# Second attention with two turned buffers and a table of inverse denominators that the output projection multiplies by

## The reference

```python
xn = layernorm(x)
q, k, v = ...                       # [B, 32 heads, S, 64], rotary positions on a part of q and k
scores = einsum('bhqd,bhkd->bhqk', q, kf) / sqrt(64)
scores = where(causal, scores, finfo.min)
attn = softmax(scores, axis=-1)
out = einsum('bhqk,bhkd->bhqd', attn, v)
out = out.transpose(0, 2, 1, 3).reshape(b, s, 32 * 64)
return out @ o_w.T
```

## Time and profile before

| | us |
|---|---|
| three runs | 2368.79, 2372.4, 2374.82 |
| median | 2372.4 |
| the profiled execution, its own time | 2372.37 |
| its span, first to last instruction | 2370.6 |
| mean granted TensorE clock (share of full speed) | 0.966 |
| attention1 | about 1030 to 1872 |
| output1 | about 1872 to 2057 |
| feed_forward1 | about 2057 to 2371 |

### The profile page before, as it was taken

How to read it: one execution, slowest core, us unless ns; L and a number is a source line. 1 busy time by engine, 2 the same in 40 slices (tenths; PEclk the granted TensorE clock), 3 DMA queues, 4 the chain that set the end, 5 groups by cost and what they waited for, 6 DMA issues and landing times. The chain is left out here.

```text
span 2370.6 us, 54461 instructions
## 1 busy us (share of the span) xinstructions
PE 2121.0 (89%) x22256; PEld 1479.6 (62%) x22256; DVE 1544.9 (65%) x2534; ACT 874.1 (37%) x1836; POOL 480.0 (20%) x408
## 2 busy tenths in 40 slices
PE   5899969999996999958898888888888699999997
PEld 4577747777775878834444444444444588787776
DVE  4544333488884544448988899988899440377776
ACT  3322113222222310025655555655656321234443
POOL 0110111212120135510111111111111344212111
PEclk9999989999998999978999999999999899999999
DMA  4221135133325543333333343333443455320100
GB/s 156 73 84 43 53 113 202 38 111 100 109 75 196 170 150 124 112 104 77 91 98 85 87 113 100 91 100 82 101 112 82 153 196 186 124 98 19 54 1 36
DMA packets 188737, 243.00 MB, mean 103 GB/s; under 512 B 38272, under 2 KB 111296, under 8 KB 185824
## 3 DMA queue, kind: packets, MB, share of 16 engines
q1 hardware_dynamic: 187648, 239.59, 32.5%
q10 hardware_dynamic: 864, 0.21, 0.0%
HBM read 156.82 MB, written 82.90 MB: 101 GB/s over the span
## 5 line engine op out<-in xcount | busy, mean ns | idle before, releaser
L1591 ACT ACTIVATE a_prob<-ps,a_nmax 128x256 f32<-128x256 f32 (+7 forms) x512 | 377.6, 740 | 353.7 <-DVE a_nmax L1619 214.0
L1704 PE MATMUL ps<-a_kt,a_q 64*128 64x512 f32 (+5 forms) x1536 | 382.8, 540 | 86.6 <-ACT a_prob L1591 63.3
L1619 DVE TENSOR_REDUCE a_nmax<-ps 128x1 f32<-128x1024 f32 (+3 forms) x256 | 257.3, 1005 | 75.7 <-PE ps L1704 74.0
L1636 DVE STREAM_TRANSPOSE a_pt_long<-a_prob 128x512 f32<-128x512 f32 (+3 forms) x512 | 279.2, 586 | 0.0
L1704 PEld LDWEIGHTS ps<-a_kt,a_q 64*128 64x128 f32 x1536 | 144.1, 194 | 186.0 <-ACT a_prob L1591 115.9
L1718 PE MATMUL ps<-a_pt_long,a_v 32*64 32x256 f32 (+3 forms) x7808 | 229.7, 346 | 1.6 <-DVE a_pt_long L1636 0.2
L1998 DVE SCALAR_TENSOR_TENSOR f_part<-ps,f_gu_scale,f_part 128x512 f32<-128x512 f32 x264 | 184.8, 746 | 65.5 <-PE ps L2045 52.2
L1718 PEld LDWEIGHTS ps<-a_pt_long,a_v 32*64 32x64 f32 x7808 | 154.3, 132 | 105.1 <-issue 76.7
L1671 POOL TENSOR_TENSOR a_o<-a_left 128x256 f32<-128x256 f32 x128 | 90.5, 729 | 597.3 <-ACT a_left L1601 597.3
L907 POOL TENSOR_TENSOR f_hT_lo<-f_h,f_hT_hi 128x512 fp32r<-128x512 f32 x64 | 82.6, 1303 | 324.5 <-ACT f_hT_hi L890 324.5
L1701 PE MATMUL ps<-a_causal,a_identb 64*128 64x128 bf16 x1024 | 112.9, 225 | 39.2 <-ACT a_prob L1591 39.2
(11 more groups left out here) (228 smaller groups left out, 4599.0 us busy)
## 6 DMA issues: line engine op xcount, KB each, us to landing
a_q<-scratch_QT SPq DMA_DIRECT2D x512, 64.0 KB, 2.1
scratch_QT<-k_qo SPq DMA_DIRECT2D x64, 256.0 KB, 2.3
a_v<-scratch_V SPq DMA_DIRECT2D x64, 256.0 KB, 4.7
scratch_OT<-a_o SPq DMA_DIRECT2D x32, 512.0 KB, 3.3
o_of<-scratch_OT SPq DMA_DIRECT2D x32, 512.0 KB, 4.1
f_block<-in_packed SPq DMA_DIRECT2D x33, 256.0 KB, 3.4
a_kt<-scratch_KT SPq DMA_DIRECT2D x128, 64.0 KB, 4.0
f_xt_hi<-scratch_xt SPq DMA_DIRECT2D x6, 1024.0 KB, 7.7
```

Source lines behind the costliest of these rows:

```text
L1591: last = nc.scalar.activation(prob[:, n % PRING, s].rearrange("p (a w) -> p a w", w=w), SC[n % 2][:, a, 0:w], ACT.Exp, bias=nmax[:, n % 4, ...
L1619: nc.vector.tensor_reduce(nmax[:, n % 4, 0:1], SC[n % 2][:, :, 0:width(0, t)], AX.XY, ALU.max, negate=True).then_inc(maxed, 1)
L1636: last = nc.vector.transpose(pt[hf][:, lo:hi, h, t - FIRST[hf], :], src.rearrange("p (j k) -> p j k", k=32))
L1704: last = pe.matmul(sc[:, a, 0:w], q[r, slot, heads[a * hf], :], kt[r, b, keys], start=not masked, stop=True, skip_group_check=True)
```

## The change

In attention1 the division goes out of the unit. ACT copies the unnormalised outputs straight from PSUM to `o` (two copies per half, `o` has two places, no `left`), and SP stores these. DVE inverts the 32 sums of a unit at once, turns the small table (`rdenT`), and SP stores it to a new array scratch_R in memory (four small transfers a unit, `store_r`). POOL has nothing to do in this stage; the constants `ones` and `diag` are not loaded.

The long turned tiles have two places (`pt_long` for blocks 0 to 23, `pt_wide` for the rest, which only tiles 7 and 6 have), so each step's tile is turned in full two steps after its score. The rings `prob` and `q` have 4 and 3 places. The tables set short values to r = 26 to 30 (steps 2 to 6 of the next unit) and long values to 34 to 46 (steps 10 to 22 of it).

In output1 each step also loads `rd` (1795 of the new code): the two rows of scratch_R that belong to the two heads of the step, each read for 64 partitions. DVE multiplies `of` by `rd` in place (1837), and ACT's rounding and SP's next loads wait for that. The first step goes in two pieces of 512 tokens.

Most of the diff of attention1 and output1 (blank lines left out):

```diff
-QRING = 4
-PRING = 8
+QRING = 3
+PRING = 4
 FIRST = (4, 0)
 BLOCKS = (32, 16)
-FRONT, BACK, WHOLE = range(3)
-TURNS = {i + 2: [(i, FRONT)] for i in range(LONG)}
-for r, back in {5: (0,), 6: (1,), 7: (2, 3), 8: (4,), 9: (5, 6), 10: (7, 8)}.items():
-    TURNS[r] += [(i, BACK) for i in back]
-for i in range(9, LONG):
-    TURNS[i + 2] += [(i, BACK)]
-TURNS.update({i + 2: [(i, WHOLE)] for i in range(LONG, USTEPS)})
-MIDDLE = 16
-LONG_VALUES = {18 + i: range(3 * i, 3 * i + 3) for i in range(10)}
-LONG_VALUES[28] = range(30, 32)
-SHORT_VALUES = {31 + i: range(2 * i, 2 * i + 2) for i in range(8)}
-LONG_LEFT = {28: (0, 1), 29: (2, 3)}
-SHORT_LEFT = {38: (0, 1), 39: (2, 3)}
-LONG_STORE, SHORT_STORE = 34, 44
-LATEST = 45
+MAIN = 24
+LATER = 2
+SHORT_VALUES = {26: range(0, 3), 27: range(3, 6), 28: range(6, 9), 29: range(9, 13), 30: range(13, 16)}
+LONG_VALUES = {34: range(0, 2), 35: range(2, 4), 36: range(4, 6), 37: range(6, 8), 38: range(8, 10), 39: range(10, 11),
+               40: range(11, 13), 41: range(13, 15), 42: range(15, 18), 43: range(18, 21), 44: range(21, 24),
+               45: range(24, 28), 46: range(28, 32)}
+SHORT_LEFT = {31: (0,), 32: (1,)}
+LONG_LEFT = {47: (0, 1)}
+SHORT_STORE, LONG_STORE = 34, 50
+INVERT = USTEPS + 2
+LATEST = 53
...
-        diag = sb("diag", [P, 32])
-        ones = sb("ones", [P, HD1])
...
-        pt = [sb(f"pt_{s}", [P, BLOCKS[i], HQ, 4, 32]) for i, s in enumerate(("long", "short"))]
+        pt_long = sb("pt_long", [P, 2, MAIN, HQ, 4, 32])
+        pt_wide = sb("pt_wide", [P, 2, BLOCKS[0] - MAIN, HQ, 2, 32])
+        pt_short = sb("pt_short", [P, BLOCKS[1], HQ, 4, 32])
-        den = sb("den", [P, 2, 16])
-        rden = sb("rden", [P, 16])
-        spread = sb("spread", [P, HQ, 4, 32])
-        left = sb("left", [P, 4, 2, 2, 4, 32])
-        o = sb("o", [P, 2, 4, 4, 32])
+        den = sb("den", [P, 2, HQ * ST])
+        rden = sb("rden", [P, HQ * ST])
+        rdenT = sb("rdenT", [P, 32])
+        o = sb("o", [P, 2, 2, 4, 4, 32])
...
+        PV_ALL = ps[:, 4 * BANK:8 * BANK].rearrange("p (i w) -> p i w", i=4)
...
+        def order(u, hf):
+            return 2 * u + (1 if hf == 0 else 0)
+        def turned_part(u, hf, j):
+            if hf:
+                return pt_short[:, j], 0
+            if j < MAIN:
+                return pt_long[:, u % 2, j], 4
+            return pt_wide[:, u % 2, j - MAIN], 6
...
+                    i = order(u, hf)
+                    sp.wait_ge(evicted, 2 * i + 2)
                     sp.dma_start(d["OT"][2 * g:2 * g + 2, :, tok:tok + 4 * P].rearrange("s p t -> p s t"),
-                                 o[:].rearrange("p s t i q -> p s (t i q)")).then_inc(o_stored, 16)
+                                 o[:, i % 2].rearrange("p s t i q -> p s (t i q)")).then_inc(o_stored[i % 2], 16)
+                def store_r(u):
+                    g, b = divmod(u, NB1)
+                    sp.wait_ge(r_turned, u + 1)
+                    for a in range(4):
+                        sp.dma_start(d["R"][g, b].rearrange("h (t a q) -> a (h t) q", t=ST, a=4)[a],
+                                     rdenT[32 * a:32 * a + 32, :]).then_inc(r_stored, 16)
...
-                for dst, src in ((diag, d["c_diag32"]), (ones, d["c_ones"])):
-                    sp.dma_start(dst[:], src).then_inc(c_in, 16)
...
                     if n >= PRING:
-                        act.wait_ge(turned, last_turn(n - PRING))
+                        act.wait_ge(turned, n - PRING + 1)
...
-                def evict(u, hf, banks):
-                    half = 2 * u + hf
-                    act.wait_ge(valued, half + 1)
-                    wait(act, o_done, 4 * half)
-                    for i in banks:
-                        nc.scalar.activation(left[:, i].rearrange("p w s t q -> p (w s t q)"), PV[i], ACT.Copy
-                                             ).then_inc(evicted, 1)
+                def evict(u, hf, pairs):
+                    i = order(u, hf)
+                    act.wait_ge(valued, i + 1)
+                    wait(act, o_stored[i % 2], 16 * (i // 2))
+                    for k in pairs:
+                        nc.scalar.activation(
+                            o[:, i % 2, :, :, 2 * k:2 * k + 2, :].rearrange("p s t i q -> p i (s t) q"),
+                            PV_ALL[:, 2 * k:2 * k + 2, 0:256].rearrange("p i (w q) -> p i w q", q=32), ACT.Copy
+                            ).then_inc(evicted, 1)
...
                     blocks = 4 * (t + 1)
-                    lo, hi = {FRONT: (0, MIDDLE), BACK: (MIDDLE, blocks), WHOLE: (0, blocks)}[part]
                     for i, h in enumerate(heads):
-                        src = prob[:, n % PRING, (i * blocks + lo) * 32:(i * blocks + hi) * 32]
-                        last = nc.vector.transpose(pt[hf][:, lo:hi, h, t - FIRST[hf], :],
-                                                   src.rearrange("p (j k) -> p j k", k=32))
+                        src = prob[:, n % PRING, i * blocks * 32:(i + 1) * blocks * 32]
+                        src = src.rearrange("p (j k) -> p j k", k=32)
+                        if hf:
+                            last = nc.vector.transpose(pt_short[:, 0:blocks, h, t, :], src)
+                        else:
+                            near = min(blocks, MAIN)
+                            last = nc.vector.transpose(pt_long[:, unit % 2, 0:near, h, t - 4, :], src[:, 0:near, :])
+                            if blocks > MAIN:
+                                last = nc.vector.transpose(pt_wide[:, unit % 2, 0:blocks - MAIN, h, t - 6, :],
+                                                           src[:, MAIN:blocks, :])
                     last.then_inc(turned, 1)
-                def invert(u, hf):
-                    half = 2 * u + hf
-                    dve.wait_ge(exped, u * USTEPS + (LONG, USTEPS)[hf])
-                    wait(dve, spread_out, half)
-                    nc.vector.reciprocal(rden[:], den[:, hf, :]).then_inc(inverted, 1)
+                def invert(u):
+                    dve.wait_ge(exped, (u + 1) * USTEPS)
+                    nc.vector.reciprocal(rden[:], den[:, u % 2, :]).then_inc(inverted, 1)
+                    dve.wait_ge(inverted, u + 1)
+                    wait(dve, r_stored, 64 * u)
+                    nc.vector.transpose(rdenT[:], rden[:]).then_inc(r_turned, 1)
...
+                    if LATER <= n < NSTEPS + LATER:
+                        turn(n - LATER)
+                    for u, r in at_step(n, (INVERT,)):
+                        invert(u)
...
-            @block.gpsimd
-            def _(pool):
-                def spread_half(u, hf):
-                    half = 2 * u + hf
-                    pool.wait_ge(inverted, half + 1)
-                    wait(pool, valued, half)
-                    nc.gpsimd.tensor_tensor(spread[:].rearrange("p h t q -> p (h t) q"),
-                                            rden[:].unsqueeze(2).broadcast_to([P, 16, 32]),
-                                            diag[:].unsqueeze(1).broadcast_to([P, 16, 32]), ALU.mult
-                                            ).then_inc(spread_out, 1)
...
-                pe.wait_ge(c_in, 16 * 6)
+                pe.wait_ge(c_in, 16 * 4)
...
-                def denominators(half):
-                    pe.wait_ge(spread_out, half + 1)
-                    for c in range(2):
-                        for i in range(4):
-                            rows = slice(32 * i, 32 * i + 32)
-                            last = pe.matmul(PV[i][c * HD1:(c + 1) * HD1, 256:512], ones[rows, :],
-                                             spread[rows, c::2, :, :], start=True, stop=True, skip_group_check=True)
-                    last.then_inc(valued, 1)
...
+                        wait(pe, evicted, 2 * order(unit, hf))
+                        if hf == 1:
...
+                    for u, r in at_step(n, SHORT_VALUES):
+                        values(u, 1, SHORT_VALUES[r])
                     for u, r in at_step(n, LONG_VALUES):
                         values(u, 0, LONG_VALUES[r])
-                    for u, r in at_step(n, SHORT_VALUES):
-                        values(u, 1, SHORT_VALUES[r])
...
+        rd = sb("rd", [P, 2, SEQ])
...
+            return [slice(i * WIDTH, (i + 1) * WIDTH) for i in range(PIECES)] if n == 0 else [slice(0, SEQ)]
+        def through(n, i=None):
+            return n + PIECES if i is None or n else i + 1
+        def landed(n, i):
+            return second_in if i else o_in[n % 3]
...
-                        sp.wait_ge(o_low, n - 2)
-                    sp.dma_start(of[:, n % 3, :], d["OT"][k, :, b * SEQ:(b + 1) * SEQ]).then_inc(o_in[n % 3], 16)
+                        sp.wait_ge(o_low, through(n - 3))
+                        sp.wait_ge(scaled, through(n - 2))
+                    for i, s in enumerate(pieces(n)):
+                        sp.dma_start(of[:, n % 3, s], d["OT"][k, :, b * SEQ + s.start:b * SEQ + s.stop]
```

(39 more changed lines are left out.)

75 lines of the change are left out of this document (22 added, 53 removed).

## The result

The changed kernel takes 2600.7 us (median of 4 runs, 2594.6 to 2607.6), the kernel before 2370.6 (4 runs). The ratio is 1.097, with a 95% interval of 1.095 to 1.100: **slower**. The forecast was 2554, with a range of 2460 to 2625. The profiled execution has a span of 2599.5 us.

The account below looks back on a forecast made before the run. In the attention neither PE nor DVE fills the time (712 and 714 of 842 us); the output projection is PE's. 2372.4 - 49 (attention) + 231 (output projection) = 2554 us, range 2460 to 2625.

Parts of the forecast that it names:

- Two engines: Output projection: each table load uses two DMA engines, 10.0 us a load, 320 us for 32; chance 0.80.
- The other loads beside it: Output projection: the stage's other 33.1 MB put a sixteenth on each of the table's two engines, 79 us.
- The unit: Attention, 24 steps of one head group of one sequence: 46.3 us against 49.9, 47.5 with low clock allowed.
- three phases: Attention unit: score 23 to 26 a chain, 4.6 us; to 34 DVE decides, 16.7; to 47 PE's values, 25.0.
- The prices: Attention: time per instruction by columns, such as 1.14 us for the longest reduce and 1.20 for a 1024-column turn.
- The start: Attention: PE no longer waits for the last constant issued at 1042, so it starts earlier: -3.5 us.
- The first two units: Attention: unit 0 has no values and takes 44 us to its score 23; each later unit takes 47.5.
- The tail: Attention's end, from the last score step to the next stage: 25.5 us against 21 today.
- the held-back turns: Old attention unit, steps 5 to 17: DVE busy 25.64 of 25.80 us, catching up turned tiles that lacked a buffer.
- Edits costed at nothing: Removing POOL's spread and scaling, ring of 4, three q buffers, and the projection's multiplication and waits: 0 us.
- Rival A: Output projection: the table load spreads over 16 engines, or as many as hide it, total 2323 us; chance 0.15.
- Rival B: Load hidden, but half-idle score-only steps drop PE's clock and the attention gains nothing, 2360 to 2400 us; chance 0.05.

Follow-up runs that it names:

- the runs with 2, 4, 8 and 64 rows: 2, 4, 8: changed kernel without table load and multiplication, plus a 512 KB load per step that nothing reads, 2582.9, 2454.3, 2389.1 us; 64: e1.
- e7: e1 with the short and long value step tables of the kernel before: 2387.7 us, ratio 1.007 to before.
- e4: e1 with the table loaded only in the first two output projection steps, all multiplications and waits kept (division wrong): 2335.9 us.
- e11: e9 plus eight products of 256 columns behind the last value block of each half, written where nobody reads: 2337.7 us.
- e1: Changed kernel with each table load split into two loads of 64 rows, same bytes: 2352.5 us, ratio 0.993 to before.
- e9: Changed attention, but the table is loaded there and POOL multiplies before the store; output projection as before the change: 2339.4 us.
- idle load of two rows: Changed kernel without table load and multiplication, plus a 512 KB load per step from two rows that no engine reads: 2582.9 us.

## Why the prediction was right, and where its sizes were off

- **Two engines** was the step that decided, taken at 0.80 on the shape alone. It held: 47 to 59 GB/s between the bursts, and 248 us that go with one edit of the load's shape. The Trainium skill ("DMA: Bandwidth & Descriptors", "Why a DMA increments its semaphore by 16 and not by 1") puts the number of engines at the largest up to 16 that divides the slowest dimension of both patterns; the runs with 2, 4, 8 and 64 rows agree in their order (stages of 431.5, 301.1, 230.7 and 201.0 us). No view here names the engines that a load used; that they are two is read from the rate and from a busy share of one tenth.
- **The other loads beside it** were mis-sized: 79 us, from the bytes at the top rate of 26.2 GB/s an engine. The earlier trace rows already had more: a share of 0.52 over 185 us is 96 us of each engine for the same bytes. In the changed kernel the share of 0.34 over 453.3 us is 154 us of each of 16; the table's 320 us on two engines are 40 of these, and 114 are left for the others. 320 + 114 + 15.5 us of start and tail are 450, with 453.3 measured. This sum is an estimate; it takes the others as spread evenly and the table at 26.2 GB/s an engine. It accounts for nearly all of the 37 us between +231 and +268. (The forecast's own terms add up to 414.5 us, not 416.)
- **The unit** was forecast at 46.3 us, and 47.5 with low clock; measured 46.5 and 47.5. By its three phases it is 4.5, 16.9 and 25.1 us in the unit behind 1473.0, against 4.6, 16.7 and 25.0. The prices are right too, though two do not follow from the working as told: 0.97 us scaled by the columns gives 1.11 for 1024 and not 1.14, and the line for turns gives 1.17 and not 1.20. The start was -3.7 us against -3.5.
- **The first two units** were the larger miss in the attention: to score 23 of unit 0 the forecast has 44 us and the trace 47.3, and from there to score 23 of unit 1 it has 47.5 and the trace 51.8, together 7.6 us more, with the clock at 0.68 and 0.85. The forecast gave unit 0 no low clock at all, though it begins behind 18 us of idle PE and though the first unit of before had a clock of 0.75. **The tail** took 28.6 us (1803.6 to 1832.2) and not 25.5. Together they are 10.7 us late; with the slightly quicker start and later units they make the 9.4 between -49 and -39.6.
- **Why the unit is shorter** was told half wrong. The forecast named the held-back turns for DVE's full stretch. Its per-step reckoning was right, since it contained both tables, but e7 shows that evening out the turns under the old value tables, together with all other edits of the attention, gives 0.5 of the 3.4 us.
- **Edits costed at nothing**: the multiplication costs some 4 us at most by the medians (e4). POOL's work and the small rings were not run by themselves; the unit's 46.5 us against 46.3 leave them 0.2 us. The denominators were counted in PE's sum, and e11 shows that in the new schedule their products are not on the path.
- **Rival A** (load over 16 engines, 2323 us) was too low: with the spread load the kernel takes 2352.5. It assumed 419 GB/s for all 49.9 MB, where e1 ran at 268. **Rival B** did not occur: the low clock costs 1.0 us a unit, as allowed.

## What to carry to other kernels

Before adding a transfer, write down the outermost count of both its patterns: a broadcast of two rows written as (2, 64, n) moved at 53 GB/s, while the same bytes as two loads of 64 rows cost 20 us in all and not 268. And add up the bytes of the stage against the rate that holds when all engines are busy (here 268 GB/s), not against the best slice; if they don't fit, move the transfer to a stage whose DMA share is low. When two engines take turns at being full, the first question is where their work stands relative to each other, before how much of it can be removed.

## What the hardware showed beside that

A load that is issued behind the narrow one is held up as well: the issue of the `gu` load lasted 9.82 us on SP's queue, where the same load took 0.59 in e1. With the idle load of two rows it took 10.37 in the median, with that of four rows 0.80. Steps 6 to 9, four steps of scores alone in which PE is idle 3.0 of 7.7 us, let the granted clock fall in six of thirteen units of e9; two more products in each of these steps kept it at 1.00.
